# The norms of the first half's hidden rows, computed with features on the partitions or with tokens on them

## What is computed

```python
def _norm(x):
    return jnp.sqrt(jnp.sum(x * x, axis=-1, keepdims=True)).clip(EPS)
def logmap0(x):
    n = _norm(x)
    return jnp.arctanh(jnp.clip(n, EPS, MAX_TANH_ARG)) * x / n
def expmap0(v):
    n = _norm(v)
    return jnp.tanh(n) * v / n
def plin(x, w, b):
    return expmap0(logmap0(x) @ w + b)
...
xm = expmap0(xn * (1 + sc_mlp) + sh_mlp)
ff = plin(plin(xm, w_f1, b_f1), w_f2, b_f2)          # w_f1: 128 x 512, w_f2: 512 x 128
ff_t = g_mlp * logmap0(ff)
return mobius_add(residual, expmap0(ff_t))
```

## Time and profile before

| | |
|---|---|
| median of three runs | 605.9 us |
| the profiled execution's own time | 606.4 us |
| its span on the core | 604.6 us |
| TensorE busy | 419.0 us (69%) |
| VectorE busy | 379.9 us (63%) |
| ScalarE busy | 238.2 us (39%) |
| mean granted TensorE clock | 0.567 of full speed |

### The profile page before, as it was taken

One profiled execution on the slowest core, in us unless ns is written; L12 is line 12 of the kernel. 1 busy time (PEld: TensorE's weight loads), 2 busy tenths in 40 slices (PEclk: granted clock), 3 DMA queues, 4 the chain that ended last, 5 costly groups with the idle time before them and its releaser, 6 DMA issues.

```text
span 604.6 us, 16158 instructions
## 1 busy us (share of the span) xinstructions
PE 419.0 (69%) x6261; PEld 324.2 (54%) x6261; DVE 379.9 (63%) x2221; ACT 238.2 (39%) x928; POOL 20.5 (3%) x31
## 2 busy tenths in 40 slices
PE   3453866687655987995367676776867674897996
PEld 2233644475544755874345454554655463676774
DVE  8888248258777656467755766667666766444442
ACT  1247866425334344234233333343343333332332
POOL 8021000000000000000000000000000000000000
PEclk9577886587555555555555555555555555556555
DMA  7300000000000000000000000000000000000000
GB/s 192 84 0 1 3 3 1 1 1 2 1 2 2 3 1 2 1 3 1 2 2 2 2 3 2 2 2 2 2 2 3 1 3 2 7 5 6 10 6 9
DMA packets 8824, 5.71 MB, mean 9 GB/s; under 512 B 1988, under 2 KB 8236, under 8 KB 8748
## 3 DMA queue, kind: packets, MB, share of 16 engines
q1 hardware_dynamic: 7564, 3.77, 2.5%
q10 hardware_dynamic: 1184, 0.92, 0.5%
HBM read 4.15 MB, written 0.52 MB: 8 GB/s over the span
## 4 chain that ended last, share of the span: by engine, by line
PE 38%; DVE 36%; ACT 19%; issue 7%; DMA 1%; ACTq 0%; DVEq 0%
PE bank L1704 15%; ACT h_fac L790 7%; DVE h_off L1342 5%; DVE pr L1335 5%; ACT gates L788 5%; PE bank L1531 5%; DVE gates L1338 4%; DVE h_fac L1336 3%; DVE mx L1275 2%; PE bank L1604 2%; PE bank L1499 2%; PE bank L1442 2%; PE bank L1506 1%; ACT ta L777 1%; PE bank L1569 1%
## 5 line engine op out<-in xcount | busy, mean ns | idle before, releaser
L1704 PE MATMUL bank<-h_off,wha 128*128 128x4 f16 x1020 | 68.8, 172 | 117.1 <-DVE h_off L1342 112.3
L1704 PEld LDWEIGHTS bank<-h_off,wha 128*128 128x128 f16 x1020 | 51.7, 109 | 172.3 <-DVE h_off L1342 168.4
L788 ACT ACTIVATE gates<-bank 128x16 f32<-128x16 f32 x256 | 47.1, 184 | 167.4 <-PE bank L1704 166.6
L1335 DVE SCALAR_TENSOR_TENSOR pr<-gates 128x8 f32<-128x8 f32 x256 | 42.4, 166 | 89.9 <-ACT gates L788 88.4
L790 ACT ACTIVATE h_fac<-gates 128x4 f32<-128x4 f32 x256 | 53.1, 207 | 113.5 <-DVE gates L1338 113.5
L1342 DVE TENSOR_TENSOR h_off<-h_fac 128x4 f16<-128x4 f32 x256 | 43.2, 169 | 63.9 <-ACT h_fac L790 63.5
L1704 PE MATMUL bank<-h_low,wha 128*128 128x4 f16 x1020 | 63.6, 167 | 0.0
L1704 PE MATMUL bank<-h_off,whb 128*128 128x4 f16 x1020 | 62.7, 166 | 0.0
L1344 DVE TENSOR_TENSOR_SCAN h_low<-h_fac,h_off 128x12 f16<-128x12 f32 x256 | 46.6, 182 | 8.7
L1531 PE MATMUL bank<-kT,qz 32*128 32x32 f32 (+7 forms) x256 | 51.1, 530 | 0.8 <-ACT kT L754 0.8
L1704 PEld LDWEIGHTS bank<-h_low,wha 128*128 128x128 f16 x1020 | 47.0, 105 | 0.0
(11 more groups left out here) (285 smaller groups left out, 731.0 us busy)
## 6 DMA issues: line engine op xcount, KB each, us to landing
x_tm<-in_x ACTq DMA_DIRECT2D x1, 512.0 KB, 5.2
x_tb<-in_x SPq DMA_DIRECT2D x4, 128.0 KB, 2.7
wf<-in_L_cond_w_f SPq DMA_DIRECT2D x2, 256.0 KB, 3.3
out_y<-tb SPq DMA_DIRECT2D x7, 64.0 KB, 2.0
ada_w<-in_L_cond_w_ada SPq DMA_DIRECT2D x1, 384.0 KB
ada_b<-in_L_cond_b_ada ACTq DMA_DIRECT2D x1, 384.0 KB, 5.8
w1s<-in_L_ffn_w SPq DMA_DIRECT2D x1, 256.0 KB
w2s<-in_L_ffn_w SPq DMA_DIRECT2D x1, 256.0 KB
```

Source lines behind the costliest of these rows:

```text
L788: nc.scalar.activation(gates[:, k, 0:GW], src, ACT.Tanh, scale=1.0 / A_SCALE).then_inc(gates_act, 1)
L1335: V.scalar_tensor_tensor(pr[:, k, :], gates[:, k, B:3 * B], 1.0, gates[:, k, 3 * B:5 * B], ALU.add, ALU.mult).then_inc(p_ready, 1)
L1704: ins = T.matmul(acc[:, g * B:(g + 1) * B], w[:, g, :], h, start=False, stop=True, skip_group_check=True)
```

## The change

For the first half, the 512 hidden values of each token are computed a second time, now with tokens on the partitions: `vT` of 128 tokens is stationary and all 512 columns of w_f1 move past it, four products into PSUM banks 2 to 5. VectorE adds the bias (which there runs along the free axis, so it needs a copy of b_f1 on every partition, loaded by one more transfer of 256 KB into the columns of `ada_b` that are no longer needed). ScalarE squares the 128x512 result in place and its accumulator gives the sum along the free axis, one column of `sm` for 128 tokens. The squares by VectorE and the 16 one-column products are gone for this half. The `f1T` path that feeds the second product stays, and the second half is as before.

```diff
+        bf1_rows = ada_b[:, 0:FF]
...
+            sp.wait_ge(adaR_ready, 1)
+            sp.dma_start(bf1_rows, spread(b_f1)).then_inc(ld_bf1, 16)
             sp.wait_ge(bias_part, 2 * BF16_PARTS - 1)
             sp.dma_start(bg_rows[:], bg_parts).then_inc(bias_ready, 16)
...                                                     (ScalarE, side(k), after up3)
+                if k == 0:
+                    for i in range(SIDE):
+                        act.wait_ge(f1_sq, i + 1)
+                        ins = nc.scalar.activation(f1q[:, i], f1q[:, i], ACT.Square, accum_out=sm[:, k, NORM_SQ, i:i + 1])
+                    ins.then_inc(f1_norm, 1)
...                                                     (VectorE, side(k), after v_ready)
-                for f in range(FC):
-                    vec.wait_ge(f1_ready, FC * k + f + 1)
-                    V.tensor_tensor(f1q[:, f], f1T[:, f], f1T[:, f], ALU.mult).then_inc(f1_sq, 1)
-                    yield f"squared{f}"
+                if k == 0:
+                    vec.wait_ge(ld_bf1, 16)
+                    for i in range(SIDE):
+                        vec.wait_ge(f1_rows_mm, i + 1)
+                        V.tensor_tensor(f1q[:, i], bank[:, 2 + i, :], bf1_rows, ALU.add).then_inc(f1_sq, 1)
+                        yield f"squared{i}"
+                else:
+                    for f in range(FC):
+                        vec.wait_ge(f1_ready, FC * k + f + 1)
+                        V.tensor_tensor(f1q[:, f], f1T[:, f], f1T[:, f], ALU.mult).then_inc(f1_sq, 1)
+                        yield f"squared{f}"
                 vec.wait_ge(f1_norm, k + 1)
-                on(V.tensor_scalar(at(A_IN), bank[:, base[0], 0:SIDE], TINY, None, ALU.max))
+                on(V.tensor_scalar(at(A_IN), bank[:, base[0], 0:SIDE] if k else at(NORM_SQ), TINY, None, ALU.max))
...                                                     (VectorE, the written order)
             until(first, "v_ready")
-            for f in range(FC):
-                until(first, f"squared{f}")
-                if f == 1:
-                    until(second, "normed0")
             until(second, "normed1")
             until(first, "f1_factor")
...                                                     (TensorE, side(k), after up3)
-                pe.wait_ge(f1_ready, FC * (k + 1))
-                for f in range(FC):
+                if k == 0:
+                    pe.wait_ge(exp_done, len(UNITS))
+                    pe.wait_ge(o_copied, 2 * NG)
+                    for c in range(SIDE):
+                        T.matmul(bank[:, 2 + c, :], vT[:, SIDE + c, :], wf1[:], start=True, stop=True).then_inc(f1_rows_mm, 1)
+                    pe.wait_ge(f1_ready, FC)
+                for f in range(FC if k else 0):
+                    if f == 0:
+                        pe.wait_ge(f1_ready, FC * (k + 1))
                     pe.wait_ge(f1_sq, FC * k + f + 1)
                     for c in range(SIDE):
                         ins = T.matmul(bank[:, base[0], c:c + 1], f1q[:, f, c * P:(c + 1) * P], ones[:, 0:1],
                                        start=(f == 0 and c == 0), stop=True, skip_group_check=True)
                     yield
-                ins.then_inc(f1_norm, 1)
+                if k:
+                    ins.then_inc(f1_norm, 1)
```

More of the change, by code:

```diff
@@ L278, in adaln_attention_lstm_ffn @@
         f1_norm = sem("f1_norm")
+        f1_rows_mm = sem("f1_rows_mm")
+        ld_bf1 = sem("ld_bf1")
         f2_mm = sem("f2_mm")
```

## The result

The changed kernel takes 602.77 us (median of five runs, 601.92 to 603.73) against 605.98 for the kernel before (five runs, 604.86 to 606.87): a ratio of 0.9947, 95% interval 0.993 to 0.9965. In a later session with twelve executions the ratio was 0.9948 (0.9925 to 0.9971).

A forecast was written before the change was run, and what follows sets the result against it. TensorE's queue was taken to bound the first half's feed-forward stage. An earlier start (0.5 us) plus down at full clock (1.6) less 0.5 handed back gave 1.6 us less: median 604.3 us, range 603.0 to 606.1.

The forecast's parts named there:

- the price of the clock in the stage: First half's feed forward: down at full instead of partly half clock takes 3.75 instead of 5.32 us, 1.6 us gained.
- What bounds the stage: First half's feed forward: TensorE alone sets the end; a microsecond won at VectorE's bias moves the program's end by one.
- Norm products out, rows in: On TensorE, 3.73 us of norm products go and four 512-column row products of 3.7 us come: no gain, no loss.
- rival 4: Slower: row products over 6 us make the factor the stage's end; 606.9 to 608.1 us; chance 0.05 for above 606.5.
- An earlier start: On TensorE, the row products start at 123.79 us instead of the norms' 124.29: 0.5 us gained.
- Down: The feed forward's second product, after the row products: about 3.75 us at full clock instead of 5.32, ending at 131.2.
- The factor's new path: Last row product, add, square, VectorE's steps: factor ready at 131.1 us, level with down's end; slack of 3.37 us used up.
- VectorE, ScalarE and the transfer: Equal VectorE work, 3.3 us of ScalarE work under waiting, and the new load landing by 30 us: all cost nothing.
- Sum at L1230: VectorE's bias instruction at the stage's end: 0.5 + 1.6 = 2.1 us earlier, 131.25 instead of 133.37 us.
- What is handed back: Behind the stage, the second half's projection and a later product may lose full clock: 0.5 us handed back.
- 3 (2.8 us): Rival, more than forecast: nothing handed back and later stretches at a better clock; 2.8 us less, 603.1 us; chance 0.1.
- The rule weighed: Skill's rule that idle gaps drop TensorE's clock: removing gapless one-column products gains nothing on down, 0.5 us instead of 2.1.

The follow-up runs named there:

- narrow: The changed kernel plus sixteen one-column products, results unused, between the row products and down; 608.22 us against 606.35 for the kernel before.
- narrow32: The changed kernel plus thirty-two one-column products, results unused, between the row products and down; stage 20.26 us in one trace, no total given.
- before_d24: The kernel before with about 2.3 us of ScalarE copies ahead of the copy the LSTM's first step waits on; 608.41 us, ratio 1.0053.
- the four wide traces: Kernel before, its first half's sixteen norm products moving 128 columns of ones instead of one; 605.54 us against 606.17, ratio 0.9989.
- wide_c: One trace of the kernel before with the first half's norm products moving 128 columns of ones instead of one; 605.65 us.
- after_d1: The changed kernel with about 1.0 us of ScalarE copies ahead of the copy the LSTM's first step waits on; 605.50 us, ratio 0.9983.

## Why the prediction was wrong

The mechanism and the sign were right; the size was not. The step that failed is the price of the clock in the stage: 1.6 us, taken from one execution in which it fell on down alone. The hand-back of 0.5 us was the second, smaller miss.

*What bounds the stage* was right: TensorE's queue. That all behind it follows at the same distance holds only for the mean (the sum of the last two columns is 463.3 us before and 463.4 changed); in one execution it is off by 0.7 to 0.9 us in either sense.

*Norm products out, rows in.* The rows were forecast at 3.7 us and took 3.60. The norms' 3.73 was mis-sized: that was one execution. In two of five they took 5.02 and 5.14 us, for the clock fell inside them, and norms and down together lost 3.3 us to it. The prediction treated the clock as a cost on down only; rival 4 even set one-column products, which "need only their loads", against products that meet the clock at full length. They do not escape it: 32 took 3.63 us at full clock in "narrow", 64 took 11.62 us in "narrow32", 2.2 us of it at full clock.

*An earlier start* of 0.5 us: the rows started 0.60 us before the last eviction ended, the norms 0.05 after; 0.65 us.

*Down* was forecast at 3.75 and took 3.73 us. Before it took 5.45 in three traces and 5.67 and 5.78 in two.

*The factor's new path* was forecast at 131.1 against down's 131.2; it came at 130.86 against 130.97. The add took 0.69 and the square 0.63 with a read of 0.19 that overlapped it. Rival 4 (factor as the end) stays unfulfilled, but the two are now within 0.11 us.

*VectorE, ScalarE and the transfer* at zero: right. The load was issued at 25.67 us and landed after 3.3.

*Sum at L1230*: 2.1 us forecast, 2.5 in the first pair (0.15 us more from the start, 0.15 from the rows, 0.1 from down), 3.2 in the mean of the traces, where the two executions with the fall inside the norms add 0.65.

*What is handed back*, 0.5 us: this failed too. It was argued from where the clock stood in one execution, and up to the first step it did go there as argued, and further (1.4 us); but the LSTM then gave 2.0, and in the other two pairs of equal clock times both signs are turned, so that 0.8 and 0.9 us are handed back. In the mean of the traces it is 0.1 us from bias to the last step. What the change does cost beside the stage, 0.3 us outside the span, was not forecast.

The traced executions differ by 2.65 us in the mean of their own times, 1.05 more than forecast: 1.1 more from the stage, mis-sized by taking one execution's clock for the rule, and 0.4 from a smaller hand-back, less 0.3 outside the span and 0.1 ahead of the stage and at the end. The other 0.55 us up to the 3.2 of the first five executions are not in these traces; the later session's medians have 2.6, so they may be chance. The rival nearest to the result was 3 (2.8 us), but by a later stretch at a better clock; in the mean of the traces that was not the cause.

*The rule weighed.* With one column moving the clock fell on a TensorE that did not idle, in all five traces of before, in "before_d24", whose stage has the same 9.13 us, and in "narrow32" (in "narrow" it did not); with 128 or 512 columns it stayed until down had ended, in the four wide traces and all four of the changed kernel. The Trainium skill's account by idle gaps ("TensorE: Matmul & The Clock Gate", "HAM oscillation — how this bites in real kernels") does not cover this case; the measurements decide against it here.

## What to carry to other kernels

A product with one moving column keeps TensorE busy in the profile but may cost its clock, and the price falls on whatever dense products stand behind it. Giving the same product 128 columns of ones cost 0.1 us here (3.84 against 3.73; the loads of the stationary blocks are busy 1.00 in every window shown of both), and kept the clock in all four traces; that it makes this kernel faster as a whole is not shown. Where a stage's length hangs on the clock, read it from several executions: measure from an event next to the stage, and do not book what happens elsewhere in one trace for or against the change. Pairs of executions whose clock changes at the same times up to the stage are the closest comparison: here three such pairs give 2.9 to 3.0 us. One microsecond of a stage can only be carried over to the total with more executions than one.

## What was not expected

The same kernel's executions differ in when the granted clock changes, and with it 439 us of LSTM become 437 and the stretch ahead of it 24.7 or 26.0, mostly in opposite senses, so that the sum moves by 1 us only; in "wide_c" both came out long. What sets the times of the changes was not tried, nor was what makes the 0.3 us outside the span: the changed kernel with a delay ("after_d1") has 1.8 us there, as before.
